# Output projection in two pieces of eight heads, with a pipeline one step shorter

## What is computed

```python
def attn_layer(x, Wqkv, qs, ksc, Wo):          # 16 heads of 64 dimensions, window 32
    q, k, v = jnp.split(x @ Wqkv, 3, -1)
    q, k, v = (sh(q), sh(k), sh(v))
    q, k = l2norm(q) * qs, l2norm(k) * ksc
    ...                                        # rotary tables with a scale
    out = local_attention(q, k, v)             # own window and the one before it
    out = out.transpose(0, 2, 1, 3).reshape(b, n, INNER)
    return out @ Wo

for i in range(DEPTH):
    x = attn_layer(shift_tokens(x), Wqkv[i], q_scale[i], k_scale[i], Wo[i]) + x
    x = ffn_layer(shift_tokens(x), ...) + x
```

## Time and profile before

| | us |
|---|---|
| median of 3 runs | 4340.46 |
| lowest, highest | 4336.21, 4341.24 |
| profiled execution | 4337.86 |
| its span, first to last instruction | 4336.0 |
| TensorE busy | 3859.4 |
| VectorE busy | 3273.3 |
| ScalarE busy | 3104.5 |
| GpSimd busy | 2502.3 |
| mean granted clock of TensorE | 0.97 |

### The profile page before, as it was taken

One profiled execution on the slowest core, in us unless ns is written; L12 is line 12 of the kernel. 1 busy time (PEld: TensorE's weight loads), 2 busy tenths in 40 slices (PEclk: granted clock), 3 DMA queues, 4 the chain that ended last, 5 costly groups with the idle time before them and its releaser, 6 DMA issues.

```text
span 4336.0 us, 101314 instructions
## 1 busy us (share of the span) xinstructions
PE 3859.4 (89%) x30950; PEld 2929.2 (68%) x31328; DVE 3273.3 (75%) x5635; ACT 3104.5 (72%) x7150; POOL 2502.3 (58%) x2247
## 2 busy tenths in 40 slices
PE   6999997899997999988999979999889999789998
PEld 4666665677765777756777657777567776577776
DVE  6877776788866888667888668887678886678876
ACT  4777776777766777757777667777577776677775
POOL 1222223777746777646777457776477774577763
PEclk8999998999998999999999999999999999999999
DMA  2111111000000000010000000000100000000002
GB/s 76 40 30 30 40 30 29 1 0 0 0 26 2 1 0 0 1 26 2 0 0 0 27 1 1 0 0 1 26 1 0 0 0 27 1 1 0 0 1 65
DMA packets 53261, 52.86 MB, mean 12 GB/s; under 512 B 13574, under 2 KB 40452, under 8 KB 51972
## 3 DMA queue, kind: packets, MB, share of 16 engines
q1 hardware_dynamic: 52996, 49.77, 4.4%
HBM read 28.77 MB, written 4.19 MB: 8 GB/s over the span
## 4 chain that ended last, share of the span: by engine, by line
PE 42%; issue 24%; ACT 17%; DVE 14%; POOL 2%; ACTq 1%; DVEq 0%; SPq 0%; DMA 0%; POOLq 0%
PE bank L357 33%; ACT sb_area L668 9%; DVE sb_ssq L1105 6%; ACT sb_area L777 4%; DVE sb_smax L1116 3%; PE bank L416 3%; PE bank L503 2%; PE bank L561 2%; PE bank L532 1%; POOL sb_area L1333 1%; ACT sb_lnb L789 1%; ACT sb_lnb L786 1%; DVE sb_xs_lo L1073 1%; DVE sb_area L1093 1%; DVE sb_nmx L1012 1%
## 5 line engine op out<-in xcount | busy, mean ns | idle before, releaser
L668 ACT ACTIVATE sb_area<-bank 128x512 f32<-128x512 f32 (+4 forms) x3029 | 1569.7, 553 | 515.3 <-PE bank L357 340.2
L357 PE MATMUL bank<-sb_area 128*64 128x64 f32 (+4 forms) x16624 | 1291.6, 274 | 95.9 <-ACT sb_area L668 57.2
L1093 DVE TENSOR_TENSOR sb_area<-bank,sb_rots 128x1024 f32<-128x1024 f32 x768 | 939.0, 1225 | 524.5 <-ACT sb_area L777 521.2
L1308 POOL TENSOR_TENSOR sb_area<-sb_area,sb_rn 128x512 f32<-128x512 f32 x768 | 785.3, 1044 | 713.2 <-ACT sb_rn L793 713.2
L1294 POOL TENSOR_TENSOR sb_area<-sb_area 128x512 f32<-128x512 f32 x768 | 970.6, 1274 | 149.1 <-DVE sb_area L1093 147.3
L357 PEld LDWEIGHTS bank<-sb_area 128*64 128x64 f32 (+2 forms) x16624 | 852.4, 152 | 202.4 <-issue 141.4
L357 PE MATMUL bank<-sb_area,sb_wvo 128*128 128x256 f32 x3072 | 728.3, 381 | 3.1 <-DVE sb_xT L1151 3.1
L357 PE MATMUL bank<-sb_wqk_hi,sb_xs_hi 128*128 128x512 f32 x768 | 398.1, 518 | 242.0 <-DVE sb_xs_lo L1073 236.6
L357 PEld LDWEIGHTS bank<-sb_area,sb_wvo 128*128 128x128 f32 x3072 | 555.0, 190 | 78.3 <-issue 12.8
L777 ACT ACTIVATE sb_area<-bank 128x512 f32<-128x512 f32 x768 | 461.3, 601 | 118.8 <-PE bank L357 113.5
L503 PE MATMUL bank<-sb_ident,sb_area 128*128 128x128 f32 x3072 | 491.4, 283 | 36.8 <-ACT sb_area L668 32.7
(11 more groups left out here) (105 smaller groups left out, 5269.2 us busy)
## 6 DMA issues: line engine op xcount, KB each, us to landing
sb_xwin<-sb_p SPq DMA_DIRECT2D x256, 64.0 KB, 2.0
sb_area<-in_Wqkv SPq DMA_DIRECT2D x7, 1024.0 KB, 5.6
sb_area<-in_WvT SPq DMA_DIRECT2D x7, 512.0 KB, 7.4
sb_wo_bd<-in_Wo SPq DMA_DIRECT2D x14, 256.0 KB, 8.3
sb_area<-in_x SPq DMA_DIRECT2D x4, 512.0 KB, 5.8
sb_area<-in_x SPq DMA_DIRECT2D x8, 256.0 KB, 2.7
x_plus_causal<-sb_area SPq DMA_DIRECT2D x8, 256.0 KB, 2.3
out<-sb_area SPq DMA_DIRECT2D x8, 256.0 KB, 3.5
```

The lines of the kernel that those rows point to most:

```text
L357: return nc.tensor.matmul(o, a, b, start=start, stop=stop, skip_group_check=True)
L668: return nc.scalar.activation(o, i, ACT.Copy)
L1093: tt_(t12[:, c % 2, :, :].rearrange("p u (h d) -> p u h d", h=8), src, bc(rots[:, tt, s, :, :], [P, 2, 8, D], 2), ALU.mult).then_inc(S["ro ...
L1308: pt_(qn[:, c, :].rearrange("p (h d) -> p h d", h=8), qsum[:, c % 2, :].rearrange("p (h d) -> p h d", h=8), r, ALU.mult).then_inc(S["qn"], 1)
```

## The change

Each pair's output projection is done in two pieces of eight heads: heads 0 to 7 in half B of the odd step 4 behind the pair's second tile, heads 8 to 15 in half A of the even step after it. LAG goes from 6 to 5, so a layer has 37 steps. The addition into `xT` comes at lag 5, in half B, behind the square sums and ahead of `rests_of_tile`; `load_next` stays in half A.

```diff
-OUT_PARTS = (((6, 3), (5, 1)), ((5, 2), (4, 0)))
-LAG = 6
+OUT_PARTS = ((5, 1), (4, 0))
+LAG = 5
...
                     def project_out(wp):
-                        for lag, k in OUT_PARTS[wp]:
-                            v = behind(t, i, part, lag)
-                            if not v or v[0] % 2 == 0:
-                                continue
...
-                            for h in range(4 * k, 4 * k + 4):
...
-                            if k == 3:
-                                m.then_inc(S["oo"], 1)
+                        lag, k = OUT_PARTS[wp]
+                        v = behind(t, i, part, lag)
+                        if not v or v[0] % 2 == 0:
+                            return
...
+                        for h in range(8 * k, 8 * k + 8):
...
+                        if k == 1:
+                            m.then_inc(S["oo"], 1)
...
                         if wp == 0:
+                            load_next()
+                        else:
                             update()
-                            load_next()
-                        elif v := behind(t, i, part, -1):
-                            rests_of_tile(*v)
+                            if v := behind(t, i, part, -1):
+                                rests_of_tile(*v)
```

More of the change, by code:

```diff
@@ L565, in project_out @@
                     def project_out(wp):
-                        for lag, k in OUT_PARTS[wp]:
-                            v = behind(t, i, part, lag)
-                            if not v or v[0] % 2 == 0:
-                                continue
[L571 to L576, removed]
-                            for h in range(4 * k, 4 * k + 4):
-                                m = mm(mbank[:, 0:256], wvo[:, h, :], ysb[:, hf, :, h * WIN:(h + 1) * WIN],
-                                       h == 0, h == HEADS - 1)
-                            if k == 3:
-                                m.then_inc(S["oo"], 1)
+                        lag, k = OUT_PARTS[wp]
+                        v = behind(t, i, part, lag)
+                        if not v or v[0] % 2 == 0:
+                            return
+                        tt, bt = v
+                        hf = tt // 2
+                        if k == 0:
+                            pe.wait_ge(S["yev0"], g_of(bt) * 8 + 2 * tt + 2)
+                            pe.wait_ge(S["yev1"], g_of(bt) * 8 + 2 * tt + 2)
+                            pe.wait_ge(S["xupd"], g_of(bt) * 2 + hf)
+                        for h in range(8 * k, 8 * k + 8):
+                            m = mm(mbank[:, 0:256], wvo[:, h, :], ysb[:, hf, :, h * WIN:(h + 1) * WIN],
+                                   h == 0, h == HEADS - 1)
+                        if k == 1:
+                            m.then_inc(S["oo"], 1)
                     if part == 2 and t == LAG + 2 * TT - 1:
```

## The result

| | us |
|---|---|
| after, median of 4 runs (lowest to highest) | 4585.88 (4584.76 to 4587.47) |
| before, median of 4 runs beside them | 4338.34 (4335.09 to 4341.24) |
| ratio, 95% interval | 1.0571 (1.0553 to 1.0589) |
| forecast, its range | 4529 (4425 to 4590) |

The kernel became 247.5 us slower, where 189 were forecast. Direction and mechanism came as predicted; the size is near the upper end of the range.

The account below looks back on a forecast made before the run. Each step was taken to begin with TensorE waiting for `xs_lo`, the end of a chain through ScalarE and VectorE. 78 pairs at 1.47 + 0.05 + 1.03 = 2.55 us give +199, drain -10: +189, hence 4529 us, range 4425 to 4590.

Parts of the forecast that it names:

- eight heads in even A: Half A of even steps: TensorE's next projection comes 1.54 us later, making `xs_lo` 1.05 us later.
- eight heads in odd B: Half B of odd steps: the next projection could come at 2617.74 against 2617.69, so +0.05 us.
- addition ahead of `xs_lo`: Half B of even steps: the update of xT stands unhidden on the chain TensorE waits for, +0.42 us.
- fall of the clock: Odd steps after an idle even step: the clock falls in 2 of 3, +1.55 us each, +1.03 expected per odd step.
- drain and the rest: End of each layer: the last piece is done 1.7 us earlier per layer, 10 us less in all.
- the slack of 0.49 us: Half B: TensorE's projection of columns 3 ends at 979.25 and ScalarE squares it only at 979.77.
- the prediction's own sign for it: Odd steps above 15.5 us with the clock at 1.00 would show that eight heads in half B do not fit.
- The likeliest case: Steady steps: the clock falls in some of the odd steps, 4529 us; chance 0.60.
- rival 1: Steady steps: the clock never falls, pairs cost 1.52 us, +109, 4449 us; chance 0.20.
- rival 2: Steady steps: the clock falls in every odd step, +229, 4569 us; chance 0.12.
- Rival 3: Half B: VectorE sets its start, so the update's leaving odd half A counts; faster, -43, 4297 us; chance 0.05.
- rival 4: Half B of even steps: ScalarE, not TensorE, sets it, and the update is hidden; about 4335 us; chance 0.03.

Follow-up runs that it names:

- clock held: Changed kernel plus four throwaway matmuls in half B of even steps, with the addition into xT moved behind `rests_of_tile`: 4461.12 us, against 4488.95 without that move.
- filling: Changed kernel plus four throwaway matmuls of 256 columns at the end of half B of even steps that have a next tile: 4488.95 us.
- the deep kernel: Changed kernel with LAG back at 6, pieces and addition left where the change puts them: 4619.48 us, ratio 1.0650 against the kernel before.

## Why the prediction was right, and where it was off

| term | forecast, us | measured, us | from |
|---|---|---|---|
| eight heads in even A | 78 x 1.05 = 82 | 87 | that edit alone |
| eight heads in odd B | 78 x 0.05 = 4 | 22 | that edit alone |
| addition ahead of `xs_lo` | 78 x 0.42 = 33 | 28 | its place, clock held |
| fall of the clock | 78 x 1.03 = 80 | 97 | with and without filling |
| drain and the rest | -10 | +13 | what is left of 247.5 |

The four measured terms add up to 234 us, though each comes from another pair of kernels: here the effects are additive. In the even step they leave nothing over: 1.15 + 0.25 + 0.33 = 1.73, where the prediction had 1.47 for it and 0.05 in the step ahead.

**The size of the piece** is the step that failed: the prediction took a piece of four at 1.54 us, from its start to the next projection, and a piece of eight at twice that, 3.08. It measures 3.26 and 3.27 (847.22 to 850.48, 856.27 to 859.54), so the four more heads cost 1.73 and not 1.54. The rows had it: 24 matmuls took 5.45 us in the earlier trace rows and 8 took 1.89 in the earlier trace rows, which is 0.22 for each one more and 1.78 for eight.

**Half A** was right in its mechanism, and the slack of 0.49 us held. With 1.73 instead of 1.54 the step comes out at 1.24 in a typical even step and 1.15 in the mean, where 1.05 was taken. **Half B of odd steps** ("The longer piece just fits") does not fit: the 0.05 read from the fill step and the 0.18 by which the piece was sized too short make 0.23, and TensorE is late by just that (0.76 behind the start of `xs_lo` instead of 0.53). The delay falls into the even step, so the prediction's own sign for it, long odd steps at a full clock, could not show it. A margin of 0.05 us should have been priced as none.

**The addition** costs 0.33 and not 0.42: its row is 0.42 long, but `xs_lo` starts 0.33 after it in after (866.47 to 866.80), since instructions of one engine overlap. The start-to-start distance is the price, not the length.

**The clock** was the largest uncertainty and came out near: falls in 55 of 72 odd steps where 2 of 3 were taken, each at about 1.6 us (72 x 1.21 / 55, by the means with and without the filling) where 1.55 was. The fill's stops of 2.0 to 2.5 us ahead of tile 4, the nearest in length, fell in five of six; a share taken from them would have been nearer. The likeliest case held; rival 1 (never, 4449 us) and rival 2 (always, 4569) did not. The time alone would have misled here: at 4586 it lies above rival 2, though 17 of 72 odd steps held, since the piece and the layers' ends cost more than forecast. It is inside the range only by the margin put on top of rival 2; the count of long steps decides between the cases. With the share known the forecast would have been 4529 + 78 x 1.55 x 0.10 = 4541. The Trainium skill, Perfetto Trace Analysis, section Matmul Optimizations, wants matmuls back to back in batches; the changed kernel has batches twice as large and a lower clock (0.947 against 0.970), with a hole where the other batch had been, and four throwaway matmuls in the hole restored it (0.971).

**The drain** was wrong in sign. The wait in the earlier trace rows did go, but from the last `xs_lo` to the last addition it takes 60.6 us after and 57.2 before. TensorE waits 1.26 and 1.32 us for ScalarE's copies in the drain where the heads of a piece stood before, and the four means now stand ahead of eight heads instead of four. Of the 3.4 us some 1.6 are a fall in the last odd step, which all six layers have. This was followed and without rows for most of its waits; "call it 1.7" had no ends, and should have had them. How the 1.8 us left over divide is not shown.

Rival 3 (faster) and rival 4 (no change) had their conditions shown false. Moving the addition out of odd half A gained nothing, odd steps being 15.15 with the clock held against 15.12 before, and even half B did not hide it (28 us). Eight heads in even half A alone cost 87 us, so TensorE does set half B when it comes that late.

## What to carry to other kernels

When a loop step begins with one engine waiting for the last link of another's chain, first look at who makes that link and whether an idler engine can make it earlier: that edit gave 4.2%, where none of the arrangements of the pieces tried here gained anything. Work that can lie anywhere should fill the places where its engine would wait, in small portions; the same work in fewer, longer portions is late in one half step and missing in the other, even where no clock falls (4322 against 4155 us for the whole change, 4426 against 4338 for one piece in half A). Size a longer portion by what one more instruction takes, not by doubling the short portion's distance to its neighbour. And an idle stretch on TensorE of 2 us in a dense loop has a price beyond itself, so ask of every piece taken out of a wait what the wait was short of.

## What the runs showed of the hardware

- A stop of 1.7 to 2.4 us of TensorE in an otherwise dense loop was followed by a granted clock below 1.00 in 55 of 72 (stops of 2.02 to 2.25), 56 of 72 (the deep kernel, 2.02 to 2.21), 38 of 72 (1.69 to 1.93) and 19 of 72 cases (2.27 to 2.38); stops of 0.29 to 0.54 and of 1.14 to 1.34 us by none. The share differs between kernels with stops of nearly the same length, the longest stops have the smallest, and no run explains it.
- A VectorE subtraction of two SBUF tiles took 0.28 us alone, and 1.24 when it started 0.18 us into a GpSimd addition; the same subtraction on GpSimd took 0.45.
- Sixteen matmuls of 256 columns took 3.26 us to the next projection, eight of them 1.54: eight more cost 1.73 (8.96 against 7.23 us from columns 0 to columns 2).
